# Splitting the second stage's quantised rows on GpSimd, with a new order of work and the down product one turn later

## The reference, cut to what matters

```python
def fp4_quant_dequant(x):
    xb = x.reshape(shape[:-1] + (shape[-1] // BLOCK, BLOCK))      # BLOCK = 16
    scale = jnp.maximum(jnp.max(jnp.abs(xb), axis=-1, keepdims=True) / 6.0, 1e-12)
    xn = xb / scale
    q = _GRID[jnp.searchsorted(_MID, jnp.abs(xn))] * jnp.sign(xn) * scale
    return q.reshape(shape)

gate = fp4_linear(x, w_gate)          # fp4_linear quantises both sides, then multiplies
y = fp4_linear(x, w_up)
h = jax.nn.silu(gate) * y             # 704 columns
out = fp4_linear(h, w_down)
```

## Time and profile before

| what | value |
|---|---|
| median of 3 runs | 1012.01 us (1011.25 to 1012.86) |
| the profiled execution's own time | 1014.64 us |
| its span in the trace | 1012.9 us |
| busy: PE, DVE, ACT, POOL | 854.3, 807.9, 494.1, 352.2 us |
| mean granted TensorE clock | 0.955 of full speed |

### The profile page before, as it was taken

One profiled execution on the slowest core, in us unless ns is written; L12 is line 12 of the kernel. 1 busy time (PEld: TensorE's weight loads), 2 busy tenths in 40 slices (PEclk: granted clock), 3 DMA queues, 4 the chain that ended last, 5 costly groups with the idle time before them and its releaser, 6 DMA issues.

```text
span 1012.9 us, 27459 instructions
## 1 busy us (share of the span) xinstructions
PE 854.3 (84%) x9542; PEld 553.8 (55%) x9542; DVE 807.9 (80%) x2157; ACT 494.1 (49%) x1177; POOL 352.2 (35%) x436
## 2 busy tenths in 40 slices
PE   3459788899999999999977898889888888988963
PEld 1246555666666666666644455555555555555532
DVE  6489989788888888888853788888888888888883
ACT  2266556567766677766643333343333333333331
POOL 0144655655655556556541111111111111111111
PEclk9589989999999999999988999999999999999995
DMA  4600000110011110111000022222222222222222
GB/s 111 195 14 20 28 27 18 36 36 28 24 34 34 34 32 19 34 34 34 26 21 12 16 53 63 61 60 52 53 58 63 63 60 60 50 56 58 63 62 58
DMA packets 110870, 47.14 MB, mean 47 GB/s; under 512 B 81713, under 2 KB 109681, under 8 KB 110804
## 3 DMA queue, kind: packets, MB, share of 16 engines
q1 hardware_dynamic: 110804, 46.22, 18.9%
HBM read 20.87 MB, written 8.54 MB: 29 GB/s over the span
## 4 chain that ended last, share of the span: by engine, by line
DVE 30%; PE 18%; issue 15%; ACT 10%; POOL 8%; DVEq 1%; POOLq 0%; ACTq 0%; DMA 0%; SPq 0%
PE bank L729 6%; POOL ffn_room L681 4%; PE bank L787 3%; DVE bank L164 3%; DVE h_value L167 2%; DVE ffn_room L1530 2%; DVE h_value L171 2%; DVE ffn_room L1544 2%; ACT h_magnet L154 2%; POOL xq L687 2%; ACT hq_split L1176 2%; PE bank L806 2%; DVE kv_bd L1383 2%; PE bank L853 2%; DVE prob L1325 2%
## 5 line engine op out<-in xcount | busy, mean ns | idle before, releaser
L681 POOL TENSOR_TENSOR ffn_room<-h_value,h_scale 128x704 f32<-128x704 f32 x32 | 44.4, 1386 | 257.9 <-DVE h_value L171 257.9
L729 PE MATMUL bank<-gu,xqT 128*128 128x512 f16 (+1 forms) x576 | 129.7, 363 | 3.6 <-DMA xqT<-xq_split 3.4
L629 POOL TENSOR_TENSOR p<-prob,p 128x520 f16<-128x520 f32 x64 | 79.2, 1238 | 58.0 <-ACT p L1069 58.0
L897 PE MATMUL bank<-wh,h 128*64 128x512 f16 x768 | 96.0, 386 | 1.8 <-ACT h L1162 1.8
L886 PE MATMUL bank<-wx,x1T 128*64 128x512 f16 x768 | 95.1, 383 | 0.9 <-DVE x1T L445 0.9
L729 PEld LDWEIGHTS bank<-gu,xqT 128*128 128x128 f16 x576 | 52.8, 100 | 63.7 <-issue 17.4
L989 PE MATMUL bank<-dn,hqT 128*128 128x256 f16 x576 | 73.2, 285 | 15.4 <-DMA hqT<-hq_split 15.4
L886 PEld LDWEIGHTS bank<-wx,x1T 128*64 128x64 f16 x768 | 78.4, 201 | 13.1 <-DVE x1T L445 1.3
L622 POOL TENSOR_TENSOR prob<-prob,row_max 128x520 f32<-128x520 f32 x64 | 69.5, 1087 | 40.4 <-DVE row_max L1333 36.4
L787 PE MATMUL bank<-ident,p 128*65 128x128 f16 x1024 | 77.7, 226 | 4.6 <-POOL p L629 4.6
L729 PE MATMUL bank<-attn,xT 128*128 128x256 f16 (+1 forms) x384 | 75.3, 337 | 0.0
(11 more groups left out here) (195 smaller groups left out, 2032.0 us busy)
## 6 DMA issues: line engine op xcount, KB each, us to landing
x_in<-in_x_columns SPq DMA_DIRECT2D x32, 128.0 KB, 2.2
x_res<-in_x SPq DMA_DIRECT2D x32, 128.0 KB, 2.1
x_rows<-x_rows_sb SPq DMA_DIRECT2D x32, 128.0 KB, 1.9
ffn_room<-x_rows SPq DMA_DIRECT2D x64, 64.0 KB, 2.2
out<-ffn_room SPq DMA_DIRECT2D x64, 64.0 KB, 2.0
mask_in<-in_mask_Bx1x1xS_ff SPq DMA_DIRECT2D x64, 16.0 KB, 2.4
x1T<-in_L_cond_Wx SPq DMA_DIRECT2D x1, 1024.0 KB, 6.3
x1T<-in_L_cond_Wh SPq DMA_DIRECT2D x1, 1024.0 KB, 8.5
```

The source lines that it names most:

```text
L629: pool.tensor_tensor(p16[:, 1, r, :], prob[:, r, :], p16[:, 0, r, :], ALU.subtract).then_inc(s["p_lo"], 1)
L681: pool.tensor_tensor(blocks(hq, FF), blocks(fp4_h.value, FF), spread(fp4_h.scale, FF), ALU.mult).then_inc(s["hq_ready"], 1)
L729: last = pe.matmul(dst, lhs(a, c), rhs(b, c), start=first and c == 0 and a == b, stop=c == C - 1 and (a, b) == parts3[-1], skip_group_chec ...
L897: last = pe.matmul(bank[e][B * h:B * h + B, :], h16[:, m, c, :], half_cols(wh16, a, c, h), start=False, stop=True, skip_group_check=True)
```

## The change

It does five things, all in the second stage.

1. The float32 product hq goes, and with it ScalarE's high part (L1176) and VectorE's low part (L1524). GpSimd now rounds the scale to bf16 (h_coarse), takes the rest (h_fine), both 128x44, and multiplies the quantised values by each, straight into the two fp16 halves of hq_split. The multiplication by h_fine stands behind the 256-wide xq on GpSimd's list. hq_split lies where hq was.
2. The down product goes one turn later (t5 instead of t4), and hqT16 has two buffers.
3. TensorE's turn is reordered: both remaining gate_up parts ahead of lstm_state(1), then down, then h_transpose(1), then the next lstm_input.
4. VectorE's and ScalarE's turns are reordered.
5. On SyncE the stores of the result go behind the transposes.

```diff
@@ -304,8 +304,10 @@
     xq = sb("xq", [P, D])
     xq_split = sb("xq_split", [P, 2, D], F16)
     xqT16 = sb("xqT16", [P, C, 2, P], F16)
-    hq_split = sb("hq_split", [P, 2, FFC * P], F16)
-    hqT16 = sb("hqT16", [P, 2, FFC, P], F16)
+    h_coarse = sb("h_coarse", [P, FF // BLK], BF16)
+    h_fine = sb("h_fine", [P, FF // BLK])
+    one_h = sb("one_h", [P, FF // BLK])
+    hqT16 = sb("hqT16", [P, 2, 2, FFC, P], F16)
 
     ffn_room = sb("ffn_room", [P, 3 * FFC * D])
     at = 0
@@ -314,9 +316,10 @@
         ffn.append(ffn_room[:, at:at + n])
         at += n
     gate_sig, silu, up_rows, hid, hq = ffn[0:5]
+    hq_split = hq.bitcast(F16).rearrange("p (a n) -> p a n", a=2)
     x1_res, out_rows = [a.rearrange("p (q d) -> p q d", q=2) for a in ffn[5:7]]
     fp4_w = {k: Fp4(sb, f"w_{k}", FFC * D, (ffn_room[:, FFC * D * i:FFC * D * (i + 1)],
-                                            hqT16[:, :, :, :].rearrange("p a k n -> p (a k n)").bitcast(BF16)))
+                                            hqT16[:, 0].rearrange("p a k n -> p (a k n)").bitcast(BF16)))
              for i, k in enumerate(FP4_JOBS)}
 
     names = """ident_zero v16_zero consts_pool consts_dve w_ps w_hi w_done bias_work bias_stored split_hi scaled_w ffn_ps ffn_hi ffn_done
@@ -328,7 +331,7 @@
         rstd_ready z_ready zg_ready xb_ready x1_ready x1_ps x1T_hi x1T_lo x1_stored
         gates_ps sig_if sig_o tanh_g i_g cell_ready tanh_c h_ready h_hi h_lo
         hT_ps magnet_w magnet_x magnet_h up_sb quant_x xq_ready xq_hi xq_lo b_passed b_zero gate_ps up_ps gate_sig_ready gate_done hid_ready
-        quant_h hq_ready hq_hi hq_lo down_ps out_ready""".split()
+        quant_h h_parts hq_hi hq_lo down_ps out_ready""".split()
     s = {name: sem(name) for name in names}
     x_loaded = sem("x_loaded")
     mask_loaded = [sem(f"mask_loaded{i}") for i in range(2)]
@@ -555,11 +558,6 @@
 
         def step(tiles):
             _, t2, _, t4, t5 = tiles
-            if t5:
-                q = t5.parity
-                sp.wait_ge(s["out_ready"], t5.count())
-                for e in range(2):
-                    sp.dma_start(out_steps[t5.number() * 2 + e], out_rows[64 * e:64 * e + 64, q, :]).then_inc(out_stored[q], 16)
             if t4:
                 q = t4.parity
                 after(sp, s["out_ready"], t4.count(back=2))
@@ -570,14 +568,19 @@
                     sp.dma_start(x1_res[64 * e:64 * e + 64, q, :], x1_steps[t4.number() * 2 + e]).then_inc(x1_loaded[q], 16)
                 for a, ready in enumerate(("hq_hi", "hq_lo")):
                     hold(sp, s[ready], t4.count(), "b_passed")
-                    hold(sp, s["down_ps"], t4.count(back=1), "b_passed")
-                    sp.dma_start_transpose(hqT16[:, a], hq_split[:, a]).then_inc(hqT_in[a], 16)
+                    hold(sp, s["down_ps"], t4.count(back=2), "b_passed")
+                    sp.dma_start_transpose(hqT16[:, q, a], hq_split[:, a]).then_inc(hqT_in[a], 16)
             if t2:
                 hold(sp, s["xq_lo"], t2.count(), "b_passed")
                 hold(sp, s["up_ps"], t2.count(back=1), "b_passed")
                 for c in range(C):
                     sp.dma_start_transpose(xqT16[:, c, :, :].rearrange("p a (e b) -> p (a e) b", e=2),
                                            xq_split[64 * c:64 * c + 64, :, :].rearrange("p a n -> p (a n)")).then_inc(xqT_in, 16)
+            if t5:
+                q = t5.parity
+                sp.wait_ge(s["out_ready"], t5.count())
+                for e in range(2):
+                    sp.dma_start(out_steps[t5.number() * 2 + e], out_rows[64 * e:64 * e + 64, q, :]).then_inc(out_stored[q], 16)
 
         pipeline(sp, 5, step, first=6)
         for q in range(2):
@@ -676,16 +679,26 @@
             _, t2, _, t4 = tiles
             if t4:
 
+                pool.wait_ge(s["quant_h"], t4.count(2, Fp4.STEPS))
+                pool.tensor_tensor(h_coarse[:, :], fp4_h.scale[:, :], one_h[:, :], ALU.mult).then_inc(s["h_parts"], 1)
+                pool.wait_ge(s["h_parts"], t4.count(1, 2))
+                pool.tensor_tensor(h_fine[:, :], fp4_h.scale[:, :], h_coarse[:, :], ALU.subtract).then_inc(s["h_parts"], 1)
                 pool.wait_ge(s["quant_h"], t4.count(Fp4.STEPS, Fp4.STEPS))
-                after(pool, s["hq_lo"], t4.count(back=1))
-                pool.tensor_tensor(blocks(hq, FF), blocks(fp4_h.value, FF), spread(fp4_h.scale, FF),
-                                   ALU.mult).then_inc(s["hq_ready"], 1)
+                after(pool, hqT_in[0], t4.count(per=16, nth=16, back=1))
+                pool.tensor_tensor(blocks(hq_split[:, 0], FF), blocks(fp4_h.value, FF), spread(h_coarse, FF),
+                                   ALU.mult).then_inc(s["hq_hi"], 1)
             if t2:
 
                 pool.wait_ge(s["quant_x"], t2.count(Fp4.STEPS, Fp4.STEPS))
                 after(pool, s["xq_lo"], t2.count(back=1))
                 pool.tensor_tensor(blocks(xq, D), blocks(fp4_x.value, D), spread(fp4_x.scale, D),
                                    ALU.mult).then_inc(s["xq_ready"], 1)
+            if t4:
+
+                pool.wait_ge(s["h_parts"], t4.count(2, 2))
+                after(pool, hqT_in[1], t4.count(per=16, nth=16, back=1))
+                pool.tensor_tensor(blocks(hq_split[:, 1], FF), blocks(fp4_h.value, FF), spread(h_fine, FF),
+                                   ALU.mult).then_inc(s["hq_lo"], 1)
 
         pipeline(pool, 4, step)
 
@@ -986,7 +999,7 @@
                 pe.wait_ge(hqT_in[part], t.count(per=16, nth=16))
                 for k in range(FFC):
                     for a, m in pairs:
-                        last = pe.matmul(dst, hqT16[:, a, k, :], dn16[:, m, k, :], start=k == 0 and (a, m) == (0, 0),
+                        last = pe.matmul(dst, hqT16[:, t.parity, a, k, :], dn16[:, m, k, :], start=k == 0 and (a, m) == (0, 0),
                                          stop=k == FFC - 1 and a == 1, skip_group_check=True)
             last.then_inc(s["down_ps"], 1)
 
@@ -996,8 +1009,8 @@
         lstm_products(Tile(None, 0), 0).then_inc(s["gates_ps"], 1)
 
         def step(tiles):
-            t1, t2, t3, t4 = tiles
-            if t1 and not (t1.loop is None and t1.b == 0):
+            t1, _, t3, _, t5 = tiles
+            if t1 and t1.b > 0:
                 lstm_state(t1, 0).then_inc(s["gates_ps"], 1)
             if t1:
                 lstm_input(t1, 1)
@@ -1007,19 +1020,18 @@
                 h_transpose(t1, 0)
             if t3:
                 gate_up(t3, 1)
+                gate_up(t3, 2)
             if t1:
                 lstm_state(t1, 1).then_inc(s["gates_ps"], 1)
+            if t5:
+                down(t5)
+            if t1:
+                h_transpose(t1, 1)
             if t1 and t1.b < NT - 1:
                 lstm_input(Tile(None, t1.b + 1), 0)
-            if t3:
-                gate_up(t3, 2)
-            if t1:
-                h_transpose(t1, 1)
-            if t4:
-                down(t4)
-
-        for n in range(NT + 3):
-            step([Tile(None, n - k) if 0 <= n - k < NT else None for k in range(4)])
+
+        for n in range(NT + 4):
+            step([Tile(None, n - k) if 0 <= n - k < NT else None for k in range(5)])
 
     @block.scalar
     def _(act):
@@ -1170,10 +1182,6 @@
                 lstm_gates(t1, 0)
                 lstm_tanh(t1, 0)
                 lstm_hi(t1, 0)
-            if t4:
-                act.wait_ge(s["hq_ready"], t4.count())
-                after(act, hqT_in[0], t4.count(per=16, nth=16, back=1))
-                act.copy(hq_split[:, 0, 0:FF], hq[:, 0:FF]).then_inc(s["hq_hi"], 1)
             if t2:
                 act.wait_ge(s["quant_x"], t2.count(Fp4.SCALED, Fp4.STEPS))
                 fp4_x.magnitude(act, D).then_inc(s["magnet_x"], 1)
@@ -1181,13 +1189,12 @@
                 act.wait_ge(s["gate_ps"], t3.count())
                 after(act, s["gate_done"], t3.count(back=1))
                 act.activation(gate_sig[:, :], wide[:, 0:FF], ACT.Sigmoid, scale=1.0 / W_G).then_inc(s["gate_sig_ready"], 1)
-            if t1:
-                lstm_gates(t1, 1)
             if t2:
                 act.wait_ge(s["xq_ready"], t2.count())
                 after(act, xqT_in, t2.count(per=32, nth=32, back=1))
                 act.copy(xq_split[:, 0, :], xq[:, :]).then_inc(s["xq_hi"], 1)
             if t1:
+                lstm_gates(t1, 1)
                 lstm_tanh(t1, 1)
                 lstm_hi(t1, 1)
 
@@ -1204,6 +1211,7 @@
         dve.memset(qk16[:, :, 3, :], 0.0)
         dve.memset(v2[:, :, P:P + 2], 1.0)
         dve.memset(cell[:, :], 0.0)
+        dve.memset(one_h[:, :], 1.0)
         dve.memset(add_mask[:, S:KEYS], 0.0)
         dve.memset(kimg16[:, :, 3, :], 0.0)
         dve.memset(vimg16[:, :, :, :], 0.0)
@@ -1502,53 +1510,48 @@
 
         def step(tiles):
             t1, t2, t3, t4, t5 = tiles
+            if t2:
+                dve.wait_ge(s["h_ready"], t2.count(2, 2))
+                after(dve, s["xq_ready"], t2.count(back=1))
```

(70 more changed lines are left out.)

## The result

The changed kernel takes 996.91 us (median of 4 runs, 993.3 to 998.38) against 1012.05 for the kernel before (four runs by now): a ratio of 0.9845, 95% interval 0.9817 to 0.9874. That is 15.1 us less, where 22.5 were forecast; it lies in the forecast range. The profiled execution has a span of 995.7.

A forecast was written before the change was run, and what follows sets the result against it. TensorE (busy 90%) and VectorE (85%) waiting for one another in a 13.66 us turn were taken as the bound. 28.1 turns of -0.70 = -19.8, +1.6 start, -4.3 end give -22.5: 1012.0 to 990 us, range 976 to 1007.

The forecast's parts named there:

- The turn: Second stage, VectorE's list: one turn falls from 13.63 to 12.92 us, 2.90 gained against 2.22 lost.
- tanh uncovered: VectorE ahead of both lstm_h: idle 0.35 us each for tanh, with the lost overlap of 0.08 costing 0.86 a turn.
- the walk: One second-stage turn written down for each engine with trace durations and gaps; the old order gives 13.63 against 13.66 us.
- The products: GpSimd's two new products in the second stage: 1.39 us each, with 1.26 to 1.59 as bounds.
- the 520-element product: A GpSimd trace row, one fp16 input and fp16 out, 1172 ns; scaled to 704 it gives 1.59 us.
- The rival with dear products: GpSimd's products eat the gain at 1.75 us each; at 2.00 the time is 1028; chance 0.10 at 1.75 or more.
- the rule of thumb: Two-input elementwise work belongs on VectorE, GpSimd being about twice as slow: products 1.75 us each, time 1012, no change.
- The blocking: VectorE's quant_x 5 and xq_lo, reading two SBUF tensors, stand until GpSimd's products end: 0.60 and 0.40 us lost a turn.
- The start: First three turns of the second stage: no FFN work to gain on, both gate_up parts ahead of lstm_state(1), +1.6 us.
- The end: Last turns of the second stage: last tile's quant_x starts at once, last transposes issue without waiting, -4.3 us.
- third rival: SyncE: hq's low half ahead of xq's transposes makes xqT late and TensorE wait; 2.3 us late gives 1018; chance 0.06.
- The cover of 1.3 us: SyncE's last xq_split transposes land at 16.4 us, the next gate_up is due at 17.7.

The follow-up runs named there:

- The PSUM experiment: The changed kernel with the magnitude of quant_x as float32 in PSUM instead of bf16 in SBUF: 984.47 us, ratio 0.9734.
- the half product: The changed kernel with GpSimd's second product over 352 of the 704 columns, the other low parts staying zero: 990.69 us, ratio 0.9807.
- the filled start: The changed kernel with the next tile's lstm_input ahead of h_transpose(1) in the first four turns, which have no down: 992.47 us, ratio 0.9795.
- the last experiment: The changed kernel with quant_x's magnitude in PSUM, the start filled by lstm_input, and lstm_cell(1) ahead of xq_lo on VectorE: 967.15 us, ratio 0.9545.
- the split alone: The kernel before, all orders as they were, with only the split moved to GpSimd (both products, the second behind xq): 1031.03 us, ratio 1.0181.
- down in the same turn: The changed kernel with down for tile t4 and last in TensorE's turn, as before the change: 1056.85 us, ratio 1.0427.

## Why the prediction was right, and where it missed

The direction, the range and the mechanism held. Point by point:

- **The turn.** 12.92 was forecast, 13.03 came. The missing 0.1 is in one term: tanh uncovered was priced at 0.35, with VectorE starting 0.03 after ScalarE's end, as the magnitude has it in the earlier trace rows. Ahead of lstm_h the wait takes 0.42, twice a turn: 58 waits between 560 and 940 us, 24.1 us in all, with VectorE starting 0.10 after tanh's end. The trace of the kernel before has both values: its fifth FFN step starts 0.03 after the magnitude's end in 12 turns, 0.10 in the other 20. With 0.42 the walk gives 13.06. The forecast of the difference was 0.70, measured 0.64.
- **The products.** 1.39 each was taken, 1.375 and 1.389 measured. The bf16 or float32 scale and the fp16 output cost nothing over the float32 product of before. (The prediction says that mixed types in one instruction are not in the trace; the 520-element product that it prices has a float32 and an fp16 input.) The rival with dear products fell with this, and so did the estimate of 1.75 by the rule of thumb. The Trainium skill (GPSIMD Engine Reference, section 3.1) gives a factor of 1.96 between the two engines, measured on an add of 2048 float32 elements; the traces differ from it for these products, with 1.39 to 0.89, that is 1.56, with the block scale read repeatedly.
- **The blocking.** Forecast: 1.02 for quant_x 5, 0.81 for xq_lo. Measured: 1.00 and 0.70; in the turn shown xq_lo starts 0.08 later than in the walk (10.82 us into the turn against 10.74), and GpSimd's product ends 0.03 earlier. The PSUM experiment shows the cause, the half product shows that it costs time. The Trainium skill says the same (SBUF — State Buffer, "Who interferes with whom"): a VectorE instruction with two SBUF inputs contends with GpSimd's reads and the later one blocks fully, and the traces agree, 0.28 behind GpSimd's end for 256 elements.
- **The start** was mis-sized: +1.6 forecast, +4.6 measured. The walk had seen that both gate_up parts delay lstm_state(1), but ran TensorE at one speed. The place left empty by down makes TensorE idle over 2 us, and behind three of the four gaps of this kind the products took longer for about 4 us (2.39 and 2.26 in the rows above instead of 1.46 and 1.49); the granted clock over two such stretches is 0.64 and 0.61, that is partly at 1.2 instead of 2.4 GHz (the windows in the last section), and 1.00 over 50 us of the filled start. The four groups of products in the two stretches took 2.39, 2.26, 2.61 and 2.05, together an estimated 3.4 us more than at the full clock, which is about the whole miss of 3.0. Filling the place took 5 us off the first turns.
- **The end**: -4.3 forecast, -2.7 measured. The last two gate_up, in a phase of waits for transposes, took 5.42 and 6.54 us at a granted clock of 0.69 and 0.56; before they took 3.74 each at 1.00. What of that comes from the change was not separated.
- **The transposes** (third rival) hardly came late: from 560 to 940 us TensorE's weight loads waited 2.4 us in all for xqT, 0.5 at most at once, and its products not at all. The cover of 1.3 us held though some of the transposes landed up to 4.1 us after their issue; with the shorter turn of the last experiment it no longer did, twice.

As a sum: -22.5 forecast; the turns gave 3.5 us less than forecast, the start 3.0, the end 1.6. That makes -14.4, and with the 2.8 us ahead of the second stage the -17.2 of the profiled pair; the medians show -15.1. Of the 3.5 about half is the price of tanh (0.06 in each of some 27 turns) and 1.2 is the turn from tile 3 to tile 4, which has the last of the four gaps. (28.1 turns of 0.70 are 19.7 and not 19.8, which changes nothing.)

What the prediction did not see is that the change's two halves are each a loss alone (+1.8% and +0.5%), and that the change took only a third of what the last kernel of this study gains: 30 us more came from a PSUM operand, one swapped pair and one filled place.

## What to carry to other kernels

Before work is moved to GpSimd, look what VectorE does while it runs there: an instruction with two SBUF inputs stands until GpSimd's ends, so an engine that is 30% busy can be on the path; put one of the two inputs in PSUM, or have instructions with a PSUM input stand there. A product moved a turn later is also a filler, and the turns that don't have it yet must get another one, or TensorE idles and may then run slow. A product that stands right behind its transpose also pays for each landing that is late. And a walk through one turn with measured durations and gaps foretells such orders well: eight expectations give a turn from it, six are within 0.12 us of the measured mean, and the two misses (the split alone, and down in the same turn) are within 0.11 on the turns that no late landing and no slower clock disturbs. Those two are what such a walk leaves out, so look at single turns and not only at their mean.

## What was not expected of the hardware

- TensorE slowed behind three of four single gaps of 2.0 to 2.9 us, with its work otherwise nearly without a break. The windows of the changed kernel behind the first three gaps, in the columns of the earlier trace rows:

```profile
551.80:556.60 4.80, 4.80 (x29) 2.62 (x31) 1.06 (x4) 0.27 (x1) 0.00 (x0) 0.64 0.02 3
564.20:567.20 3.00, 3.00 (x30) 2.21 (x30) 1.06 (x4) 0.33 (x2) 0.00 (x0) 1.00 0.11 22
576.30:580.70 4.40, 4.40 (x28) 2.33 (x28) 3.65 (x9) 1.01 (x2) 0.55 (x2) 0.61 0.18 45
```

  The engine is busy all through each, and the granted clock is 0.64 behind the gap of 2.04, 1.00 behind that of 2.85, the longest, and 0.61 behind that of 2.14. So the length of the gap alone doesn't decide. In the filled start, with gaps of 0.5 to 1.3, it stays at full:

```profile
553.00:603.00 50.00, 42.65 (x312) 25.01 (x309) 38.89 (x98) 18.44 (x59) 9.56 (x14) 1.00 0.18 38
```

  The kernel with down in the same turn has a gap of 2.0 to 2.9 us in each of its 32 turns. Behind 16 of them the granted clock fell to the lower level, in all but one case 0.7 to 1.5 us after the end of the gap, and behind the other 16, with gaps just as long, it stayed at full. What tells the two kinds of gap apart, no run here shows.
- A transposing DMA that lands in 2.3 or 2.7 us at the median took 3.3 to 4.8 now and then, in every kernel of this study. It costs nothing where no product waits for it, and made two turns at the full clock 1.7 and 1.8 us longer where one does (15.56 and 15.71 against 13.89, the split alone). What makes it late, no run here shows.
- VectorE takes up a result of ScalarE either 0.03 or 0.10 us after its end. It is 0.10 at each wait for tanh ahead of lstm_h in the changed kernel, 0.03 at 12 and 0.10 at 20 of the magnitudes of quant_h in the kernel before, with VectorE idle in both. That tan_c lies in PSUM isn't the reason: with quant_x's magnitude in PSUM it is 0.03 at 24 of 32 magnitudes, and 0.03 at 24 of 31 with it in SBUF. What decides between the two, no run here shows.
